# Recurrent cell by pairs of heads from halves split on chip, gates in one product, and value products moved forward in the grouped attention

## The reference

```python
ig = (concat([q, k, v]) @ igate_w.T + igate_b).T         # one row of gates a head
fg = (concat([q, k, v]) @ fgate_w.T + fgate_b).T
cs = cumsum(log_sigmoid(fg), axis=1)
log_D = where(tril, cs[:, :, None] - cs[:, None, :], -inf) + ig[:, None, :]
D_mat = exp(log_D - max(log_D, -1))
C = einsum('hsd,htd->hst', qh, kh) / sqrt(32) * D_mat
normalizer = maximum(abs(C.sum(-1)), exp(-max_log_D))
h = einsum('hst,htd->hsd', C / (normalizer + 1e-6), vh)  # then layernorm of h, times ln_scale
```

## Time and profile before

| what | us |
|---|---|
| three runs: median (lowest, highest) | 7131.78 (7130.37, 7140.3) |
| the profiled execution: its own time | 7131.68 |
| its span | 7130.0 |
| stage `cell_gates` | 124 |
| stage `a4` (`qkv` with the identity) | 148 |
| stage `cell` | 437 |
| stages t1, t3, t7 | 496, 479, 321 |

### The profile page before, as it was taken

The page is one execution under the profiler, slowest core; times in us unless marked ns, Lnnn a source line. Parts: engine busy times, 40 slices in busy tenths (PEclk is TensorE's granted clock), DMA queues, the critical chain, the costliest instruction groups (busy, mean ns, idle before and its releaser), DMA issues. The chain is left out here.

```text
span 7130.0 us, 108835 instructions
## 1 busy us (share of the span) xinstructions
PE 4954.3 (69%) x25218; PEld 2892.3 (41%) x25218; DVE 4005.8 (56%) x8286; ACT 2764.5 (39%) x5926; POOL 1940.0 (27%) x2979
## 2 busy tenths in 40 slices
PE   6344666492777873996667476767767696885897
PEld 3112333240442332882312264556655483222543
DVE  6223555537546765442656696644966455785464
ACT  2223555015225632221234255632555431662252
POOL 0002443000025620220022255411554123451242
PEclk9556888695888986998878798988989897998697
DMA  4888996100052321110466133110332005231543
GB/s 148 224 243 202 190 187 160 44 0 0 0 174 77 89 51 42 41 42 25 133 122 116 40 121 112 60 32 24 109 119 78 28 11 187 77 82 47 165 120 90
DMA packets 503550, 679.98 MB, mean 95 GB/s; under 512 B 102218, under 2 KB 323052, under 8 KB 503105
## 3 DMA queue, kind: packets, MB, share of 16 engines
q1 hardware_dynamic: 437384, 504.19, 24.4%
q0 software_dynamic: 65792, 171.82, 10.7%
HBM read 402.70 MB, written 254.56 MB: 92 GB/s over the span
## 5 line engine op out<-in xcount | busy, mean ns | idle before, releaser
L1110 DVE TENSOR_REDUCE t_nmax<-t_aps 128x2 f32<-128x1024 f32 x700 | 851.4, 1223 | 366.4 <-PE t_aps L1037 352.3
L1215 ACT ACTIVATE t_expT<-t_bps 128x512 f32<-128x512 f32 x1290 | 672.9, 601 | 295.9 <-PE t_bps L1056 267.7
L1056 PE MATMUL t_bps<-t_Q,t_K 51*128 51x512 f32 (+2 forms) x1290 | 462.7, 476 | 127.8 <-ACT t_expT L1215 103.4
L1037 PE MATMUL t_aps<-t_K,t_Q 49*128 49x512 f32 (+2 forms) x1400 | 422.8, 449 | 63.1 <-DMA t_K<-k_halves 28.5
L2386 DVE TENSOR_TENSOR f_hl<-f_h,f_hh 128x512 fp32r<-128x512 f32 x192 | 203.9, 1062 | 423.2 <-ACT f_hh L2317 423.2
L1086 PE MATMUL t_ops<-t_expT,t_V 128*17 128x512 f32 (+1 forms) x2560 | 408.8, 606 | 0.0
L3711 ACT ACTIVATE t_relsb<-t_relsb,t_nmax 128x128 f32<-128x128 f32 (+3 forms) x515 | 279.5, 560 | 311.3 <-DVE t_nmax L3684 307.3
L1056 PEld LDWEIGHTS t_bps<-t_Q,t_K 51*128 51x128 f32 (+2 forms) x1290 | 185.2, 188 | 521.5 <-ACT t_expT L1215 394.4
L3645 PE MATMUL t_tps<-ident,t_relsb 128*128 128x128 f32 x1280 | 261.6, 312 | 173.4 <-ACT t_expT L3530 165.9
L3359 ACT ACTIVATE t_prob<-t_summed,t_nmax 128x256 f32<-128x256 f32 (+1 forms) x552 | 261.1, 474 | 303.7 <-DVE t_nmax L3410 303.7
L2674 POOL TENSOR_TENSOR a_crossed<-a_qsb,a_tab 128x256 f32<-128x256 f32 x272 | 263.5, 991 | 308.3 <-ACT a_qsb L2620 279.1
(11 more groups left out here) (419 smaller groups left out, 12618.8 us busy)
## 6 DMA issues: line engine op xcount, KB each, us to landing
rel<-r_out SPq DMA_DIRECT2D x128, 256.0 KB, 2.1
t_relsb<-rel SPq DMA_DIRECT2D x128, 256.0 KB, 5.0
t_Q<-q_halves POOLq DMA_DIRECT2D x420, 64.0 KB, 2.6
t_K<-k_halves POOLq DMA_DIRECT2D x420, 64.0 KB, 2.6
rel<-r_out SPq DMA_DIRECT2D x128, 192.0 KB, 1.9
t_relsb<-rel SPq DMA_DIRECT2D x128, 192.0 KB, 3.6
k_halves<-a_parts SPq DMA_DIRECT2D x48, 512.0 KB
q_halves<-a_parts SPq DMA_DIRECT2D x48, 512.0 KB, 5.4
```

The source lines that it names most:

```text
L1037: last = nc.tensor.matmul(aps[:, (t * PPG + i) % 2, x, :], operand(Qr, KA, p, h, slice(t * P, (t + 1) * P)), operand(Kr, KA, p, h, slice(0 ...
L1056: nc.tensor.matmul(bps[:, slot_of(kb, j), :], operand(Kr, KB, p, h, slice(kb * P, (kb + 1) * P)), operand(Qr, KB, p, h, slice(0, S)), star ...
L1110: nc.vector.tensor_reduce(nmax[:, g, t, i * HPT:(i + 1) * HPT], aps[:, (t * PPG + i) % 2], AX.X, ALU.max, negate=True).then_inc(s["maxed"], 1)
L1215: nc.scalar.activation(expT[:, kb % RING, j, :], bps[:, slot_of(kb, j), :], ACT.Exp).then_inc(s["expo"], 1 + (PAD if end else 0))
```

## The change

Six things change.

1. `cell_gates`: both gates stand in one weight matrix of 16 columns, so 6 products a sequence instead of 12, one bias instruction instead of two, and the DMAs that change the layout are issued as each sequence is done.
2. The stage `a4` is gone, with its DRAM copies of queries, keys and values.
3. `cell` gets the transposed stream in SBUF and loads the context itself. ACT rounds queries and keys to fp32r (`Qh`, `Kh`), POOL subtracts to get the rest (`Ql`, `Kl`, 128x1024 each), PE turns the context into values, and scores are three fp32r products, Kh Qh + Kl Qh + Kh Ql, on the 32 rows of a head.
4. `cell` goes by pairs of heads, written out for all 32 pairs. The two heads' products alternate: scores on different groups of rows, value products in different groups of columns. Value products run one pair behind the scores, `keep` and `turn` two behind, `divide` three behind, and the normalisation of a sequence is spread over the third pair of the next.
5. `grouped_attention`: in each step the value products go before the last `turned` and the last `scores`. On DVE the last `maxima` goes behind the copy of `ops`.
6. `grouped_attention`, prologue: POOL's first splits stand between the loads of the second sequence, instead of behind them.

```diff
@@ grouped_attention, PE @@
-                    for i in range(PPG):
-                        for x in range(HPT):
-                            turned(p1, G1, g1, kb1, i * HPT + x)
-                        scores(p2, G0 + DEPTH, g2, kb, i)
...
+                    for j in range(HG - 1):
+                        turned(p1, G1, g1, kb1, j)
+                        if j == 1:
+                            scores(p2, G0 + DEPTH, g2, kb, 0)
+                    products()
+                    turned(p1, G1, g1, kb1, HG - 1)
+                    scores(p2, G0 + DEPTH, g2, kb, PPG - 1)
@@ grouped_attention, DVE @@
-                    for i in range(PPG):
+                    for i in range(PPG - 1):
                         maxima(G0 + DEPTH, g2, kb, i)
...
                         nc.vector.tensor_copy(osb[:, p, g, :], ops[:, :]).then_inc(s["o_free"], 1)
+                    maxima(G0 + DEPTH, g2, kb, PPG - 1)
@@ grouped_attention, POOL @@
-                for g in range(NG):
-                    load(1, g, 1)
-                values(1, 1)
                 for g in range(DEPTH):
...
                     split(g, g, g % 2)
+                    load(1, g, 1)
@@ cell_gates @@
-                        for W, o in ((WI, ips), (WF, fps)):
-                            for j in range(6):
...
+                    for j in range(6):
...
+                        last = nc.tensor.matmul(gps[0:2 * H, b % 2, :], W[:, j, :], x, start=j == 0, stop=j == 5)
...
+                for b in range(NB):
+                    sp.wait_ge(s["raw"], b + 1)
+                    sp.dma_start(ig[b * H:(b + 1) * H, :], raw[0:H, b * S:(b + 1) * S]).then_inc(s["lay"], 16)
@@ cell, SP @@
+                for g in range(2, NP):
+                    b, i = pair(g)
+                    sp.wait_ge(s["d"], (g - 1) * NT)
+                    maxima(g)
@@ cell, POOL @@
+                    nc.gpsimd.tensor_tensor(fast(Ql[:, b % 2]), xT[:, :, b * S:(b + 1) * S], Qh[:, b % 2], ALU.subtract).then_inc(s["ql"], 1)
...
+                for g in range(NP):
+                    b, i = pair(g)
+                    diagonal(g)
+                    if i == 1 and b + 1 < NB:
+                        queries(b + 1)
+                    if i == 2 and b + 1 < NB:
+                        keys(b + 1)
+                    if i == 3 and b:
+                        spread(b - 1)
@@ cell, PE @@
+                def scores(b, i, k):
...
+                    wait(pe, "ct", u - 1)
+                    for n, (x, y) in enumerate(((Kh, Qh), (Kl, Qh), (Kh, Ql))):
+                        for j in range(2):
+                            r, kt = (2 * i + j) % 4 * DH, (2 * i + j) // 4
+                            last = nc.tensor.matmul(sps[:, k % 2 * 2 + j, 0:WIDTH[k]], fast(x[r:r + DH, b % 2, kt, k * P:(k + 1) * P]),
+                                                    fast(y[r:r + DH, b % 2, kt, k * P:S]), start=n == 0, stop=n == 2)
...
+                def step(b, i, k):
+                    g = b * HP + i
+                    if b < NB:
+                        scores(b, i, k)
+                    if 1 <= g <= NP:
+                        products(g - 1, k)
+                    if k == 1 and i >= 2 and b + 1 < NB:
+                        values(b + 1, i - 2)
+                    if k == NT - 1 and 2 <= g <= NP + 1:
+                        turn(g - 2)
@@ cell, DVE @@
+                def step(b, i, k):
+                    g = b * HP + i
+                    if k == 0 and 3 <= g <= NP + 2:
+                        divide(g - 3)
+                    if k == 1 and 2 <= g <= NP + 1:
+                        keep(g - 2)
+                    if b < NB:
+                        weigh(b, i, k)
@@ program @@
-                eye = (w_view(a["c_eye"]), [P, KT, D])
-                qkv(nc, G, "a4", G.X,
...
+                cell(nc, G, "t4", xT, a["ctx_T"], Mrow, gT, eT, a["L2_xattn_ln_scale"], 2)
```

More of the change, by code:

```diff
@@ L1185, in _ @@
                     split(g, g, g % 2)
+                    load(1, g, 1)
+                for g in range(DEPTH, NG):
+                    load(1, g, 1)
+                values(1, 1)
                 with pool.Fori(0, NB // 2 - 1) as it:
@@ L2931, in cell, with fast, steps, wait @@
         mv = sb("mv", [P, NT, 2])
+        var = sb("var", [P, NT])
         rstd = sb("rstd", [P, NT])
-        Vh = sb("Vh", [P, 2, NT, DA])
-        osb = sb("osb", [DA, H, S])
-        sps = ps("sps", [P, 2, S])
-        hps = ps("hps", [DA, 2, S])
-        ops = ps("ops", [P, NT, S])
+        sps = ps("sps", [P, 4, S])
+        hps = ps("hps", [P, 2, S])
+        ops = ps("ops", [P, 2, S])
+        def fast(x):
+            return x.bitcast(F32R)
+        def steps(step):
+            for b in range(NB):
+                for i in range(HP):
+                    for k in range(NT):
+                        step(b, i, k)
+            for i in range(3):
+                for k in range(NT):
+                    step(NB, i, k)
+        def wait(eng, what, n):
+            if n > 0:
+                eng.wait_ge(s[what], n)
+        def pair(g):
+            return g // HP, g % HP
         with nc.Block() as block:
@@ L3014, in _ @@
+                queries(0)
+                keys(0)
+                pool.wait_ge(s["tri"], 1)
+                for g in range(NP):
[7 more added lines that the diff above has]
+                        spread(b - 1)
+                spread(NB - 1)
             @block.tensor
@@ new lines, in products @@
+                def products(g, k):
+                    b, i = pair(g)
+                    pe.wait_ge(s["ct"], g * NT + k + 1)
+                    if k == 0:
+                        pe.wait_ge(s["vcp"], 2 * b + 2)
+                        pe.wait_ge(s["zero"], 1)
+                        wait(pe, "kept", g - 1)
+                    for j in range(2):
+                        last = nc.tensor.matmul(hps[j * 64:j * 64 + DA, g % 2, k * P:S], V[:, b % 2, k, 2 * i + j, :], C[:, i, j, OFF[k]:OFF[k] + WIDTH[k]],
+                                                start=k == 0, stop=k == NT - 1, skip_group_check=True)
+                    if k == NT - 1:
+                        last.then_inc(s["pv"], 1)
@@ new lines, in turn @@
+                def turn(g):
+                    b, i = pair(g)
+                    pe.wait_ge(s["kept"], g + 1)
+                    if i == 2 and b + 1 < NB:
+                        pe.wait_ge(s["vcp"], 2 * b + 4)
+                    else:
+                        wait(pe, "normed", g - 1 - (0 if i < 2 else 1) - (2 if i == 2 else 0))
+                    for t in range(NT):
+                        last = nc.tensor.transpose(ops[:, TURN_SLOT[i], t * P:(t + 1) * P], osb[:, g % 2, t * P:(t + 1) * P], G.ident[:, :])
+                    last.then_inc(s["turned"], 1)
@@ L3083, in _ @@
+                queries(0)
+                keys(0)
+                for kt in range(KT):
+                    values(0, kt)
+                steps(step)
             @block.vector
             def _(dve):
-                ch = Chain(dve, s["dvc"])
-                dve.sem_inc(s["ct"], NT)
-                dve.sem_inc(s["out_free"], 1)
+                nc.vector.memset(hps[:, :, :], 0.0).then_inc(s["zero"], 1)
+                nc.vector.tensor_scalar(eT[:, :, :], eT[:, :, :], EPS, None, ALU.add)
```

415 lines of the change are left out of this document (196 added, 219 removed).

## The result

| | before | after |
|---|---|---|
| median of the runs (lowest, highest), 4 each | 7134.87 (7130.37, 7140.3) | 6773.83 (6757.27, 6785.71) |
| ratio, 95% interval | | 0.9492 (0.9476, 0.9508) |
| profiled execution: its time (span) | 7131.68 (7130.0) | 6757.27 (6755.6) |

The change makes the kernel faster by 5.1%, 361 us between the medians, 374 between the two profiled executions. I had forecast 472. The median lies inside the range of 6590 to 6780, near its slow end, and outside the likeliest case's own range (6615 to 6710); one of the four runs, 6785.71, lies outside the range.

The account below looks back on a forecast made before the run. Chains of waits between engines bound most stages, the cell included; only t7 had PE nearly full. Terms 56 + 148 + 172 + 80 - 21 + 37 = 472 took 7131.7 to 6660, range 6590 to 6780.

Parts of the forecast that it names:

- Gates: Gates stage: fewer instructions, PSUM waits covered and DMAs issued under the products; 56 us less (50 to 60).
- Cell: Cell stage: 7.35 us a pair of heads on DVE, cell 265 us, 172 less (cell 245 to 330).
- PE: ... Sum 6.4: Cell, PE's work per pair of heads: scores 2.8, value products 2.6, transposes 1.0; 6.4 us (5.5 to 9.5).
- DVE bounds, with PE close behind it: Cell: DVE's 6.9 us a pair sets the pace, PE's 6.4 close; with the wait for `turn`, 7.35.
- rival A: Cell: PE bounds, as two heads' scores don't overlap or drains eat it; 9.2 a pair, cell 322, time 6717; 15%.
- t1 and t3: Attention stages t1 and t3: a group falls from 12.6 to 11.4 us; 80 us less together (0 to 120).
- Rival B: t1 and t3 gain nothing, DVE being within 0.1 of the chain; 80 less gained, time 6740; chance 12%.
- t7: Attention stage t7: a chain of 2.3 us a step replaces PE's 2.10; 21 us more (0 to 30).
- Prologues: Attention prologues: POOL's earlier splits remove PE's idle time before the first shift; 37 us less (28 to 38).
- C: t1 and t3 run at DVE's 10.6 a group, t7 stays at 2.10 a step; time 6588 to 6610; chance 11%.
- D: Cell: engines follow each other for each pair, 27.8 us a pair; slower than before, time 7315; chance 2%.
- I am wrong if the cell is over 300: Sign against the forecast: cell over 300 us, with t7 not slower or a t1 group over 12 as alternatives.

Follow-up runs that it names:

- c_rows64: After, with each head's three score products over 64 rows instead of 32, two heads side by side; 6674.12 us, ratio to before 0.9359.
- c_rows128: After, with every score product over all 128 rows, so one after another on one tile; 6709.36 us, ratio to before 0.9392.
- attn_only: Before, with only the change of the attentions (PE's order, DVE's order, POOL's prologue); 7040.01 us, ratio to before 0.9864.
- f_best: After, with scores over 64 rows padded by zeros, masked keys brought by DMA, and before's order in t7; 6680.52 us, ratio to before 0.9366.

## Why the prediction was right, and where it was wrong

**Gates: right.** 60 for 56. ACT's bias instructions now come every 5.15 us (0.68 and the idle 4.47 in the row; 5.2 forecast), and from the last of them to DVE's start it is 3.4, not 5.5:

```profile
3270.61 0.68 ACT L2861 ACTIVATE g_raw<-g_gps,g_bias 16x512 f32<-16x512 f32 x1 [4.47 <-PE g_gps L2847]
```

```profile
3273.97 0.42 DVE L2882 TENSOR_SCALAR g_t<-g_fg 64x512 f32<-64x512 f32 x1 [50.11 <-DMA g_fg<-g_raw]
```

**`a4`: right**, 148.

**Cell: the mechanism wrong, its sizes right at the clock I had assumed.** The step that failed is "PE: ... Sum 6.4", and with it "DVE bounds, with PE close behind it". PE's durations of products came from rows in which PE ran at the upper level, and the prediction has no term for the clock at all: it takes that level for granted, where before's cell had 0.81 with a PE less busy. At the upper level the sum is good: c_rows64 has PE 7.0 a pair (6.4), DVE 7.1 (6.9), ACT 5.5 (5.9), POOL 4.2 (4.2), and a cell of 274 where I had 265, with DVE the fullest and, as forecast, `divide` waiting for `turn` at the head of a pair. In after PE has 10.8 a pair (345.5 by 32), because 0.50 stands where I had 1.00. Nothing in the rows before showed fp32r on 32 rows, as I had written, and I had asked of it only whether two tiles overlap, not what it does to the clock. PE is the bound, as in rival A, and beyond A's 322, but not for A's reason: the heads' scores do overlap. The six products of 512 columns take 0.90 us at the upper level; one after another on 128 rows they take 1.57 in c_rows128:

```profile
3427.28 0.71 PE L3044 MATMUL t_sps<-t_Qh,t_Kh 128*128 128x512 f32 x2
...
3428.85 1.05 PE L3056 MATMUL t_hps<-t_C,t_V 128*33 128x512 f32 x4
```

The Trainium skill (TensorEngine Tiling (Array Packing), Key Properties) says that different tiles can work in parallel, and these two numbers agree. The same section says that a change of the tiling mode drains TensorE; no run shows that drain apart.
**t1 and t3: the step right, a piece given back.** 11.4 forecast; the copies of `ops` in t3 are 11.5 apart:

```profile
5780.89 0.69 DVE L1131 COPY t_osb<-t_ops 128x512 f32<-128x512 f32 x1
5792.41 0.69 DVE L1131 COPY t_osb<-t_ops 128x512 f32<-128x512 f32 x1
...
6016.92 0.69 DVE L1131 COPY t_osb<-t_ops 128x512 f32<-128x512 f32 x1
6034.42 0.69 DVE L1131 COPY t_osb<-t_ops 128x512 f32<-128x512 f32 x1 [0.80 <-PE t_ops L1083]
```

The last two are 17.5 apart. That is where the code's loop turns, after every eighth group, and there the clock falls:

```profile
6010.00:6020.00 10.00, 8.85 (x57) 2.92 (x56) 8.73 (x8) 6.39 (x13) 5.13 (x13) 1.00 0.27 75
6020.00:6038.00 18.00, 17.08 (x68) 6.02 (x68) 10.30 (x9) 10.74 (x20) 7.51 (x16) 0.53 0.42 107
```

At the six turns of t1 and t3 a group took 13.7 to 15.9 before and takes 14.0 to 17.5 now. The clock was low at one of them before and at all six after, for 3.4 to 17.1 us. In attn_only, with the same order, it was low at four of the six; in its t1 the group at a turn took 12.8 where the clock stayed up (twice) and 15.3 where it fell. So the new order does not bring the fall at every turn, and in t1 the fall is 2.5 us of such a group. Over 12.7 and 11.5 for a plain group, the turns cost 8 us before and 21 after, which is 13 of the missing 19. From the first to the last copy t1 went from 399.7 to 365.2 and t3 from 396.5 to 369.7: 61 for 80. Rival B (no gain) is out. Whether DVE or the chain sets the 11.5 was not tried.

**t7: the direction right, the size wrong.** Groups of 8.92 for 8.68, 8 us and not 21. I had put 0.2 on each step. The starts of the value products show that a plain step costs what it did and the one with the shift pays:

```profile
6503.67 1.05 PE L1083 MATMUL t_ops<-t_expT,t_V 128*33 128x512 f32 x4
...
6505.84 1.05 PE L1083 MATMUL t_ops<-t_expT,t_V 128*33 128x512 f32 x4
...
6506.82 0.50 PE L1056 MATMUL t_bps<-t_Q,t_K 98*128 98x512 f32 x1
...
6507.36 0.60 ACT L1222 ACTIVATE t_expT<-t_bps 128x512 f32<-128x512 f32 x1 [0.73 <-PE t_bps L1056]
...
6508.01 1.05 PE L1083 MATMUL t_ops<-t_expT,t_V 128*33 128x512 f32 x4
```

2.17 and 2.17, where 8.68 / 4 is 2.17 as well; three of these and one of 2.41 make 8.92. The chain is there, but shorter than my 2.3: products 0.98 (6505.84 to 6506.82), `turned` to its exponential 0.54 (6507.36), exponential 0.60, semaphore 0.05 (6508.01). The 0.66 that I had used for the second piece came from a row in which two `turned` are merged. Chain and PE's work are equal, and only the shift's step is longer. f_best takes the old order there and has 8.68 again, so the loss is the order's. It put PE's products and DVE's copy back together, so that only the chain in the rows, and no run, tells which of the two it was.

**Prologues: right.** The first shift comes right behind the last first scores:

```profile
2134.02 1.02 PE L1047 MATMUL t_bps<-identr,t_mparts 128*8 128x128 f32 x8
```

From the first scores to the first shift it is 26.6, 26.6 and 15.5 us, where it was 46.7, 40.0 and 21.0: 39 for 37.

**Chances and range.** Of the rivals, C and D are out, B is out, and A had the right bound for the wrong reason. By the forecast's own sign, "I am wrong if the cell is over 300", its main term is wrong: the cell is 366. The range reached to 6780 on account of A and B, neither of which came, and held 6774 by 6 us: that is luck.

**Slips in the working.** ACT's four copies are 3.6 by their own price and not 3.4 (they take 3.2 in after). Rival A's 9.2 a pair gives a cell of 324 and not 322, the bound of 9.5 gives 334 and not 330, and DVE's 2.62 a step gives 10.5 a group and not 10.6. The 0.28 was called a price on whole rows; the rows show 98 and 96. None of them changes a case.

## What to carry to other kernels

A duration from a row holds only at the clock of that row: before adding up PE's time for a new stage, ask not only whether PE stays busy but whether what it does there has been seen to raise the clock again after a pause. Where packing small products on few rows makes PE the bound at a low PEclk, try the same products on more rows, padded with zeros, or one short burst of full products behind each pause. And read PEclk in every stage of the changed kernel first; a busy PE at 0.50 looks like a full engine and is half of one.
